# One of four softmax normalisations of the second attention block moved from VectorE to GpSimd

## The reference

```python
q = (x @ q_w + q_b).reshape(B, LQ, H, HD).transpose(0, 2, 1, 3)     # 8, 16, 100, 32
k = (encoder_hidden_states @ k_w + k_b).reshape(B, LK, H, HD).transpose(0, 2, 1, 3)
v = (encoder_hidden_states @ v_w + v_b).reshape(B, LK, H, HD).transpose(0, 2, 1, 3)
scores = jnp.where(mask, jnp.einsum('bhqd,bhkd->bhqk', q, k) * scale, mask_value)
attn = jax.nn.softmax(scores, axis=-1)                                # 8, 16, 100, 361
out = jnp.einsum('bhqk,bhkd->bhqd', attn, v)
```

## Time and profile before

| | us |
|---|---|
| median of 3 runs | 2166.14 (2164.07 to 2168.86) |
| the profiled execution, its own time | 2166.27 |
| its span (first to last instruction) | 2164.5 |
| outside the span | 1.8 |
| second attention in it, from its first logits to the last units' exponentials | 1711.7 to 2001.4 |
| busy over the span (page) | PE 97%, DVE 61%, ACT 52%, POOL 39% |

### The profile page before, as it was taken

How to read it: one execution, slowest core, us unless ns; L and a number is a source line. 1 busy time by engine, 2 the same in 40 slices (tenths; PEclk the granted TensorE clock), 3 DMA queues, 4 the chain that set the end, 5 groups by cost and what they waited for, 6 DMA issues and landing times.

```text
span 2164.5 us, 34597 instructions
## 1 busy us (share of the span) xinstructions
PE 2092.4 (97%) x11872; PEld 1975.0 (91%) x11872; DVE 1319.0 (61%) x3268; ACT 1119.1 (52%) x2520; POOL 845.7 (39%) x770
## 2 busy tenths in 40 slices
PE   7999999999999999999999999999999999897999
PEld 6899999989999999999999999999999888786999
DVE  6657476665747756574765657476446487688241
ACT  5444456444444644444554444455466476567454
POOL 5143353624335352433536243441666211032364
PEclk9999999999999999999999999999999999999999
DMA  5654435464454554545455454545354667764243
GB/s 154 204 129 136 137 99 94 134 203 127 127 145 106 108 146 135 127 134 138 100 110 150 128 139 138 131 117 112 103 157 113 176 166 183 187 185 130 71 130 115
DMA packets 236812, 293.33 MB, mean 136 GB/s; under 512 B 113249, under 2 KB 164577, under 8 KB 236641
## 3 DMA queue, kind: packets, MB, share of 16 engines
q1 hardware_dynamic: 236640, 291.14, 50.0%
HBM read 258.84 MB, written 28.95 MB: 133 GB/s over the span
## 4 chain that ended last, share of the span: by engine, by line
PE 84%; DVE 4%; ACT 4%; DMA 3%; SPq 2%; issue 2%; POOL 1%; ACTq 0%; DVEq 0%; POOLq 0%
PE bank L1064 78%; PE bank L1173 3%; DMA k_parts<-kT 2%; PE bank L1138 1%; SPq L820 1%; POOL mring L974 1%; ACT prob L1593 1%; DVE QU L1775 1%; DVE prob L1963 1%; PE bank L1344 1%; SPq L809 1%; DVE pT L1775 0%; ACT qs L1477 0%; ACT mring L1477 0%; ACT prob L1599 0%
## 5 line engine op out<-in xcount | busy, mean ns | idle before, releaser
L974 POOL TENSOR_TENSOR mring<-stage,mring 128x512 fp32r<-128x512 f32 x389 | 516.0, 1332 | 357.7 <-ACT mring L1477 337.4
L1064 PE MATMUL bank<-pT,ctxN 128*128 128x500 f32 (+3 forms) x2304 | 467.5, 351 | 1.2 <-DVE pT L1775 1.2
L1064 PE MATMUL bank<-ctxT,QU 128*125 128x362 f32 (+1 forms) x2496 | 455.6, 333 | 11.9 <-DVE ctxT L1775 9.3
L1064 PEld LDWEIGHTS bank<-ctxT,QU 128*125 128x125 f32 (+1 forms) x2496 | 418.2, 186 | 23.7 <-DVE ctxT L1775 11.0
L1775 DVE TENSOR_TENSOR QU<-bank,QU 128x400 fp32r<-128x400 f32 (+2 forms) x512 | 276.7, 570 | 245.6 <-ACT QU L1477 245.1
L1064 PEld LDWEIGHTS bank<-pT,ctxN 128*128 128x128 f32 (+1 forms) x2304 | 371.9, 189 | 36.8 <-DVE pT L1775 1.4
L1019 POOL TENSOR_TENSOR ctxN<-ctxN_raw,ctxN 128x384 fp32r<-128x384 f32 x144 | 146.8, 1031 | 529.9 <-ACT ctxN L1477 529.9
L1064 PE MATMUL bank<-hT,mring 128*128 128x400 f32 x1656 | 329.8, 349 | 7.1 <-ACT hT L1477 6.4
L1477 ACT ACTIVATE QU<-bank 128x400 fp32r<-128x400 f32 (+2 forms) x512 | 240.3, 502 | 170.6 <-PE bank L1064 167.8
L1064 PEld LDWEIGHTS bank<-hT,mring 128*128 128x128 f32 x1656 | 304.8, 190 | 15.6 <-issue 7.3
L1477 ACT ACTIVATE pT<-bank 128x375 fp32r<-128x375 f32 (+2 forms) x336 | 152.5, 454 | 260.5 <-PE bank L1173 238.8
(11 more groups left out here) (111 smaller groups left out, 2654.2 us busy)
## 6 DMA issues: line engine op xcount, KB each, us to landing
ctxT<-c_parts SPq DMA_DIRECT2D x84, 724.0 KB, 5.7
ctxN_raw<-in_ctx SPq DMA_DIRECT2D x192, 192.0 KB, 2.7
k<-k_parts SPq DMA_DIRECT2D x96, 181.0 KB, 3.4
stage<-in_wq SPq DMA_DIRECT2D x64, 256.0 KB, 2.6
stage<-in_wk SPq DMA_DIRECT2D x64, 256.0 KB, 3.0
stage<-in_wv SPq DMA_DIRECT2D x64, 256.0 KB, 2.6
stage<-in_wo SPq DMA_DIRECT2D x64, 256.0 KB, 2.9
stage<-in_fa SPq DMA_DIRECT2D x64, 256.0 KB, 2.6
```

What stands on the lines that cost most here:

```text
L974: nc.gpsimd.tensor_tensor(lo, src, f32(hi), ALU.subtract).then_inc(S.w_ready, 1)
L1064: mm = pe.matmul(dst, parts_l[a], parts_r[b], start=first and k == 0, stop=last and k == len(order) - 1)
```

## The change

GpSimd takes the normalisation of the units with i = 3. A semaphore `p1_pool` counts them, `turn1` waits for it at those units, and VectorE keeps i = 0 and 2. GpSimd's 32 new tasks have the due times 304 + s + 0.95 and the priority 9. `rden`, the buffers and all other orders stay.

```diff
+        S.p1_pool = sem("p1_pool")
...
+        def by_pool(u):
+            return u % HG == 3
+
+        def by_vector(u):
+            return u % HG in (0, 2)
...
+            def normalise1(u):
+                k = u % PB
+                pool.wait_ge(S.rden1_ready, u + 1)
+                x = prob1[0:LQ, k, 0:LK]
+                nc.gpsimd.tensor_scalar(x, x, rden[0:LQ, k:k + 1], 1.0, ALU.mult, ALU.mult).then_inc(S.p1_pool, 1)
+
...
+            extra += [(T_ATT1 + s + 0.95, 9, normalise1, HG * s + HG - 1) for s in range(NS)]
             extra.sort(key=lambda e: e[:2])
...
             def turn1(u):
                 if by_act(u):
                     pe.wait_ge(S.p1_act, u // HG + 1)
+                elif by_pool(u):
+                    pe.wait_ge(S.p1_pool, u // HG + 1)
                 else:
-                    pe.wait_ge(S.p1_ready, u + 1 - (u + HG - 1) // HG)
+                    pe.wait_ge(S.p1_ready, u // 2 + 1)
...
-                    if 0 <= u - 1 < NU1 and not by_act(u - 1):
+                    if 0 <= u - 1 < NU1 and by_vector(u - 1):
                         normalise1(u - 1)
```

## The result

| | before | changed |
|---|---|---|
| median of 6 runs each, us | 2164.40 | 2173.35 |
| lowest and highest, us | 2162.22, 2168.86 | 2172.05, 2178.03 |
| profiled execution and its span, us | 2166.27, 2164.5 | 2172.05, 2170.3 |

The ratio is 1.0042 with a 95% interval of 1.0031 to 1.0053: slower by 9 us (6.7 to 11.5), where +8.0 and 2174.2 were forecast.

A forecast was written before the change was run, and what follows sets the result against it. TensorE was taken to pace most of the second attention and VectorE its end, with SyncE's DMA chain in steps 8 to 15. Stops 8.7 + clock 0.8 - relief 1.5 = +8.0 us, 2174.2 us; 8-in-10 range 2168.5 to 2181.

The forecast's parts named there:

- the relief: VectorE sheds 32 normalisations: 1.2 us gained in steps 29 to 31 and 0.3 us in other waits, 1.5 us.
- The faster rival: Relief for VectorE wins: waits for its low copy and the backlog shrink, 6 us, time 2161; chance 0.05.
- the rival in which slack swallows the stops: SyncE's chain absorbs unit 27's stop and a similar chain unit 11's: +2.7 us, 2168.9; chance 0.15.
- The order of GpSimd's queue: In steps 2, 6, 19, 23, 27 the row queues behind a layer norm's task: stops of 10.7 us, 8.7 arriving.
- Unit 27: Step 6's row behind norm_scale(7): stop of 3.2 us, 0.7 absorbed, 2.5 into SyncE's DMA chain.
- unit 111: Step 27's row behind norm_scale(8): stop of 3.2 us, TensorE paces, all 3.2 arriving.
- unit 95: Step 23's row behind norm_square_sum(8): stop of 1.1 us, 0.1 arriving because TensorE later waits for the context.
- Unit 11: Step 2's row behind norm_square_sum(7): stop of 2.3 us, 2.0 arriving.
- Unit 79: Step 19's row behind norm_sum(8): stop of 0.9 us, TensorE paces, all 0.9 arriving.
- The clock: Half speed of TensorE after long stops: 0.8 us, from 0 to 3.4 for both open stops; unit 27's covered.
- Shared access: GpSimd's new instruction sharing memory with VectorE: costed at nothing; 1.3 us over the last three steps if cover goes.
- The last three steps: Steps 29 to 31, paced by VectorE: some 22 us instead of 23.2, if the clock does not fall there.

The follow-up runs named there:

- E4: Changed kernel with the normalisation of the i = 3 rows left out, done by nobody: median 2162.89 us, ratio 0.9991 to the kernel before.
- E3: Changed kernel with only 27 rows on GpSimd; VectorE keeps those of steps 2, 6, 19, 23, 27: median 2163.32 us, ratio 0.9990 to before.
- E10: E1 with the rows of units 28 and 112 moved from VectorE to ScalarE: ratio 1.0005 to the kernel before.
- E1: Changed kernel with GpSimd's rows due earlier, ahead of the layer norm's tasks: median 2165.17 us against 2165.57 before, ratio 1.0006.
- E2: Changed kernel with only the rows of steps 2, 6, 19, 23, 27 on GpSimd: median 2174.80 us, ratio 1.0039 to the kernel before.
- E5: E3 with GpSimd working twice on each of its 27 rows: median 2168.69 us against 2166.81 for the kernel before, ratio 1.0008.
- E6: Changed kernel with only unit 27's row on GpSimd, VectorE doing the other 95: ratio 1.0008 to the kernel before, 1.7 us.
- E8: Changed kernel with GpSimd taking ScalarE's i = 1 rows, ahead of the norms' tasks, VectorE keeping its 96: ratio 0.9994 to the kernel before.

## Why the prediction was right, point by point

**What bounds the stage.** Right. E4 puts the most that VectorE can give at 2 us, and the terms had 1.5. From step 28 to the end the kernels with the relief and no stop or held row (E3, E4, E10) took 193.3 us, those with neither relief nor stop 195.1: the 1.8 us lie at the stage's end, as forecast. The faster rival is excluded by E4, and the rival in which slack swallows the stops (+2.7 us) by the change's interval of 6.7 to 11.5 us.

**The order of GpSimd's queue.** Right, and the core of it. Forecast stops of 2.3, 3.2, 0.9, 1.1 and 3.2 us, 10.7 together; measured 2.30, 2.82, 0.82, 1.56 and 2.92, 10.4. Unit 27's and unit 111's were shorter since GpSimd's four adds took 4.14 and 4.13 us instead of 4.29 and 4.27, the way from their end to the transpose 0.61 instead of 0.66, and TensorE became free 1.93 and 1.82 us after their start instead of 1.78 and 1.77; unit 95's was longer, since TensorE's wait for the low copy in front of it had gone. E1, E2 and E3 show the cause: take the order away and the loss is gone, do only those five and it is there.

**GpSimd's instruction.** 0.57 us, not 0.50. E5 shows that this hardly matters.

**What of the stops arrives.** Unit 11: steps 3 to 6 took 38.9 us with it and 36.5 in seven kernels without it, 2.4 us against my 2.0. (In the profile before, half clock cost 1.2 us of that stretch already.) Unit 27: 2.4 on average against 2.5, but by a way that I had partly wrong: I said that half speed behind this stop is covered. It is not; it delays the last logits of step 7, for which SyncE's load of keys waits. The changed kernel's load went at 1779.59, 11.2 us after the start of step 7, where it had gone at 1777.04, 7.4 us after it: 3.8 us later and not 2.5. And the stop before unit 64's logits shrank to 5.92 us, not to 5.5. How much of that comes through is open, since the stretch itself varies by 3.8 us between kernels without the stop; that the average comes so near my 2.5 is luck. Unit 79: step 20 took 9.17 us instead of 8.14, 1.0 against 0.9. Unit 95: step 24 took 0.5 us more and step 25 1.0 less, which fits the forecast that it is absorbed; but without a stop these steps vary from 8.6 to 9.8 and from 7.7 to 12.5 us, so it is not shown. Unit 111: from step 28 to the end the changed kernel took 3.7 us more than E3, E4 and E10, and E2, without relief, 3.8 more than before and E6, for stop and clock against 3.2 + 0.8.

Together 2.4 + 2.4 + 1.0 + 3.7 = 9.5 us, and less the relief of 1.8 some 7.7, where 9 were measured, from 6.7 to 11.5. Neither this sum nor the forecast's +8.0 is told apart from the measurement, and part of the closeness is luck: the stops were a little shorter than forecast and the clock behind them cost more. The two profiled executions are only 5.8 us apart, since the changed one was the fastest of its six.

**The clock.** The term was 0.8 for the open stops, and all three long ones brought 3.4 us at half clock; step 3's excess is 3.35 us for a stop of 2.30, step 7's 4.6 for 2.82, step 28's 4.1 for 2.92 (against E4). So the clock took 1.0, 1.8 and 1.2 us in those steps. The term had 0.8 for units 11 and 111 together and nothing for unit 27: it was too small by 1.4 us in the steps of the first two, and wrong in its reason for the third.

**Shared access.** I costed it at nothing for the row on GpSimd, and that holds: E3 does as well as E4. But I took 0.83 us as the price of a VectorE normalisation beside GpSimd's adds; E1 shows 2.47. And E5 and E8 show that the price is paid more often when GpSimd has more to do: in the kernel before and in both of them the normalisations beside no GpSimd instruction average 0.41 us, and every one over 0.6 us lies beside one. The Trainium skill (GPSIMD Engine Reference, Specifications) tells of this contention for VectorE instructions in a two-port mode or with two SBUF inputs, without a size. The trace agrees as to who suffers: the normalisation did, while maxima, reciprocals and low copies, which read PSUM or a single column, did not (0.52, 0.15 and 0.45 us in E10's rows above). That the normalisation is one of the instructions that the page names is not shown by any run.

**The last three steps.** Forecast some 22 us, if the clock held. It did not. The same 20.7 us stretch from the start of step 29, before and then changed:
```profile
1978.20:1998.90 20.70, 13.77 (x75) 9.83 (x73) 18.40 (x62) 15.00 (x43) 7.62 (x8) 0.92 0.44 126
```
```profile
1986.10:2006.80 20.70, 16.58 (x76) 12.87 (x75) 17.28 (x59) 15.67 (x44) 9.32 (x11) 0.71 0.48 134
```
The mean granted clock fell from 0.92 to 0.71, and VectorE had 1.1 us less to do in the same time. From the first logits of step 29 to the last ones of the stage it was 20.64 us before and 19.85 changed.

## What to carry to other kernels

An engine that is 16% busy is not free: it runs its queue in order, and before a latency-critical task is put there, look at what stands ahead of it and what that waits for; place it before tasks that wait for the end of the same step. Cost a long stop of TensorE as its length plus the half clock behind it (here 1.0 to 1.8 us behind stops of 2.3 to 2.9 us, nothing behind 0.8 and 1.6), and ask of the queue that paces the stage whether it waits for TensorE behind the stop. Then measure the ceiling by leaving the work out: here it was 0.1%, so even the perfect move was hardly worth a semaphore.

## What was not expected of the hardware

One VectorE multiplication of 100x361 in SBUF, with a scalar column, was held for 2.47 us, until 0.2 us after GpSimd's run of four two-input adds was over, twice in one profile; in the kernel before, the like one took 0.83 us beside the same adds. The short one began during the first add and ended at 1772.83, 0.20 us after that add's end at 1772.63. The long one began during the second and was not let in behind it, nor behind the third (1770.78), but only behind the fourth (1771.76). Why it is once the one and once the other was not tried.

GpSimd's multiplication of 100x361 took 0.57 us with a scalar from a column and 0.50 us with a constant, against VectorE's 0.41.
